# Dealing out the expert work anew in a fused two-layer network: earlier loads, a row of ones on another engine, and a band stage that starts in halves

## The chip, the cores and the metric

The program runs on one core of one Trainium2 chip. The time is device microseconds of one launch. The unchanged kernel took 1212.18 us as the median of three runs (1210.66 to 1214.54). Engines are named as in the profile: PE is the matmul engine, DVE the vector engine, ACT the scalar engine, POOL the GpSimd engine, SP the engine that here only issues DMAs.

## The reference, cut to what matters

Two layers over x of shape (4, 512, 128). Only the first is touched by the change:

```python
# first layer: windowed attention, 16 heads, a window of 64 earlier tokens
strain = disp_win - disp[:, :, :, None, :]
bond_act = gelu(strain @ W_strain + rel_emb @ W_pos)            # exact gelu
damage_act = gelu(strain @ W_dmg + b_dmg)
damage = sigmoid((damage_act @ W_dmg_out)[..., 0] + b_dmg_out[0])
logits = (bond_act @ W_bond)[..., 0] - 10.0 * damage
out = einsum('bntd,bntde->bnte', softmax(masked logits), val_win) @ W_cproj
# first layer: mixture of 16 experts, each token goes to 4 of them
route = softmax over the top 4 of t @ gate_w.T + gate_b
acc += route[e] * (swiglu(t @ mlp1_w[e].T + b1[e]) @ mlp2_w[e].T + b2[e])
# second layer: full attention with 16 heads, and 8 experts with 2 per token
```

## The kernel before, in words

The first layer is six blocks one after the other; at the end of a block all engines meet at a barrier. They are: a setup (0 to 40 us), a loop for heads 0 to 7 (`g` = 0, from 40), a band stage for them (from 331), the same loop for heads 8 to 15 (`g` = 1, from 414), its band stage (from 682), and then, from 776, the second layer.

**The loop.** A loop works through 64 window positions ("items"), 8 to each of its 8 iterations `it`. For one item DVE forms the two strained inputs (`strain`, L757, one of 2.2 us for the bond and one for the damage half), ACT takes the gelu (L895, or L900, L901 and L903), and PE reduces the result to logits (`reduce`, L957) and gives back the ring buffer. In 5 of 8 items PE forms the damage half instead of DVE (`strain` of PE, L981 and L985) from a bf16 copy `DS` of the input in three parts, whose partitions 96 to 98 hold ones for a bias. At the start of each loop DVE and ACT split the input in three parts (L863, L870, L935, L937), SP copies them to `DS` (12 DMAs, L669), and POOL writes the ones (L732). At the end of each half iteration ACT takes a tanh of the logits (`tanh`, L911).

**Experts between the items.** The expert rows of the first layer lie in 20 groups of 512 rows, sorted by expert. POOL scatters the rows of all tokens to them by 64 indirect DMAs (L741) during the first loop. A group then takes these steps: SP loads its rows (`tokens`, L649) and its weights (`weights1`, L656; `weights2`, L663); PE turns the rows (`turn`, L1019); DVE copies them (`move_in`, L813); PE multiplies by the first weights (`hidden`, L1027); DVE adds the bias (`glu_in`, L821), ACT takes a tanh (`sig`, L917), DVE combines (`glu_out`, L828); PE multiplies by the second weights (`expert_out`, L1036); DVE copies the result out (`move_out`, L835); and POOL works out where the rows go (`goals`, L712 to L718) and scatters them by 4 indirect DMAs (`store`, L723). An iteration has room for two groups, A and B_. The table `MOE_ITS` says which iterations have groups: 5, 6 and 7 of the first loop (groups 0 to 5), and 0 to 6 of the second (groups 6 to 19). The `turn` of an iteration's A stands at the end of the iteration before. SP issues all of these DMAs in the order in which they are written, so a wait of one holds back the rest. At the end of the second loop SP waits for all stores and starts to load the results back (`fetch`, L592).

**The band stage.** Four blocks `k` of 128 tokens. PE turns the logits, DVE subtracts the maximum (L1163, L1165), ACT takes the exponential into `zs` (`weigh`, L1212), SP writes `zs` to DRAM (`write`, L1138, 1 MB), and SP and POOL read it back shifted by one token per row (`read`, L1121, SP the first 64 rows of a block, POOL the others). Then PE turns what came back (`turn`, L1298), DVE and ACT copy it (L1174, L1238), and PE gathers the values (L1316, L1324). For block 0 the exponential is taken in two halves of the groups of heads (`parts_of`), but the write and the read are whole. Before block 0's turn PE fills its time with `keep_busy` (L151, 20 matmuls), which works on nothing.

Of the kernel before, what the change touches and what calls it, by code (L numbers as in the profile page):

```python
# [20 lines left out]
P = 128  # L21
# [4 lines left out]
WIN = 64  # L26
# [34 lines left out]
MOE_ITS = ((5, 6, 7), (0, 1, 2, 3, 4, 5, 6))  # L61
# [41 lines left out]
def moe_groups(g, it):  # L103

    if it not in MOE_ITS[g]:
        return None, None
    first = 2 * (len(MOE_ITS[0]) * g + MOE_ITS[g].index(it))
    return first, first + 1
# [79 lines left out]
def first_layer(nc, t_in, l0, sb, psum, sem, ident, ACC, nhalf, stats, mv, rstd, carried):  # L188
# [55 lines left out]
    with ExitStack() as su:  # L244
# [333 lines left out]
        sem(n) for n in ("moe_turned", "moe_moved", "h_ready", "xg_ready", "sig_ready", "s_ready", "y_ready", "y_used"))  # L578
    d_scatter, d_w2, goals_ready = sem("d_scatter0"), sem("d_w2_"), sem("goals_ready")
# [34 lines left out]
    for g in range(G):  # L614
        with ExitStack() as lp:
# [25 lines left out]
            groups = [n for it in MOE_ITS[g] for n in moe_groups(g, it)]  # L641

            @block.sync
            def _(sp):
# [20 lines left out]
                sp.wait_ge(small_pool, 5 + 2 * g)  # L665
# [15 lines left out]
                first, end = groups[0], groups[-1] + 1  # L681
                weights1(first)
# [16 lines left out]
                for n in range(2):  # L699
                    sp.wait_ge(d_ys[n], 64 * (end // 2))  # L700
# [5 lines left out]
            def _(pool):  # L706
# [25 lines left out]
                pool.memset(DS[96:99], 1.0).then_inc(small_pool, 1)  # L732
                pool.wait_ge(small_pool, 6 + 2 * g)
# [17 lines left out]
            def _(v):  # L751
# [85 lines left out]
                def body(it):  # L837
                    A, B_ = moe_groups(g, it)
                    before = moe_groups(g, it - 1)[1]
# [44 lines left out]
            def _(act):  # L884
# [33 lines left out]

                def body(it):
# [1466 lines left out]
```

## Time and profile before

| | |
|---|---|
| median of three runs | 1212.18 us |
| the profiled execution | 1208.67 us, of which its span is 1206.9 us |
| mean granted clock of PE | 0.928 of full speed |
| PE, DVE, ACT, POOL busy | 83%, 75%, 65%, 48% of the span |

The profiled execution is 3.5 us below the median of the runs. Times in the rows further down are microseconds from the start of its span. A row of the timeline reads: start, time, engine, line, operation, what it writes and reads, how often in a row, and in brackets how long its engine had stood idle before it and what ended that.

### The profile page before, as it was taken

To read this page: it belongs to the slowest core of one execution; us is meant where nothing else is said; L and a number is where in the kernel's file an instruction comes from. 1 tells how busy PE (TensorE), PEld (TensorE's weight loads), DVE (VectorE), ACT (ScalarE), POOL (GpSimd) and SP (SyncE) were. 2 spreads that over 40 slices of the span, in tenths; PEclk is the share of its full clock that TensorE was granted. 3 is DMA by queue.
4 is the path that set the end of the run, shared out by engine and by line. 5 is a ranking of instruction groups with operands and counts; after the bars stand their busy time and mean duration, and the time that the engine had idled before them with its cause. 6 is when DMAs were issued, how large, how long until landed. Compare 5 with 4: busy or idle time off the path is not lost. (4 is left out here: it accounts for less than half of the span.)

```text
span 1206.9 us, 24564 instructions
## 1 busy us (share of the span) xinstructions
PE 998.7 (83%) x9762; PEld 543.5 (45%) x9762; DVE 905.2 (75%) x1050; ACT 781.6 (65%) x840; POOL 573.5 (48%) x568
## 2 busy tenths in 40 slices
PE   6677787699569649999998687899999999999898
PEld 3422222233268514433333386753654565646533
DVE  7888788599363579999999674667768577576756
ACT  3589999599453459999999652143156666665464
POOL 5598888258555234888887510232760000000072
PEclk9779999799879869999999978999879999999999
DMA  8470100112157132222221396000132344522121
GB/s 302 122 271 32 36 31 31 45 49 67 38 161 188 24 84 59 72 73 70 70 70 33 100 254 142 24 1 1 36 105 62 105 132 124 155 84 84 47 59 45
DMA packets 117101, 105.14 MB, mean 87 GB/s; under 512 B 11551, under 2 KB 103419, under 8 KB 116347
## 3 DMA queue, kind: packets, MB, share of 16 engines
q1 hardware_dynamic: 106968, 83.24, 24.4%
q0 software_dynamic: 8448, 20.13, 5.9%
q8 instruction: 77, 1.26, 0.5%
q10 hardware_dynamic: 1571, 0.20, 0.1%
q14 instruction: 37, 0.30, 0.1%
HBM read 62.05 MB, written 38.34 MB: 83 GB/s over the span
## 5 line engine op out<-in xcount | busy, mean ns | idle before, releaser
L757 DVE SCALAR_TENSOR_TENSOR ring<-AD,PT 128x1808 f32<-128x1808 f32 (+15 forms) x128 | 282.1, 2221 | 33.2 <-PE LG L957 30.8
L957 PE MATMUL LG<-ring,lred 128*32 128x456 f32 (+15 forms) x2048 | 242.9, 595 | 17.6 <-ACT ring L895 17.6
L723 POOL DMA_INDIRECT ys<-yo,goali x80 | 168.5, 2107 | 77.8 <-DVE yo L835 54.7
L895 ACT ACTIVATE ring<-ring 128x3616 f32<-128x3616 f32 (+15 forms) x52 | 177.3, 3410 | 14.9 <-DVE ring L757 14.8
L2222 DVE TENSOR_REDUCE MX<-SS 128x2 f32<-128x1024 f32 x119 | 144.5, 1218 | 55.8 <-PE SS L1939 55.7
L2152 ACT ACTIVATE EX<-SS 128x1024 f32<-128x1024 f32 x128 | 130.4, 1031 | 78.9 <-PE SS L1939 78.4
L741 POOL DMA_INDIRECT xs<-rows,sloti x64 | 142.5, 2227 | 23.7 <-issue 19.2
L981 PE MATMUL SD<-DS,eyes 99*32 99x456 bf16 (+14 forms) x1216 | 92.0, 379 | 61.4 <-ACT ring L900 61.0
L901 ACT ACTIVATE ring<-ring 128x1824 f32<-128x1824 f32 (+14 forms) x76 | 139.0, 1829 | 0.0
L1856 POOL DMA_INDIRECT XN<-ys,sloti x16 | 16.2, 1015 | 248.0 <-PE SS L1949 243.5
L957 PEld LDWEIGHTS LG<-ring,lred 128*32 128x32 f32 x2048 | 62.0, 113 | 122.5 <-issue 93.3
L757 DVE SCALAR_TENSOR_TENSOR ring<-AD,bdmg 128x1808 f32<-128x1808 f32 (+15 forms) x52 | 114.8, 2207 | 0.0
L900 ACT ACTIVATE ring<-SD 128x912 f32<-128x912 f32 (+14 forms) x76 | 74.7, 983 | 33.6 <-PE SD L985 32.7
L981 PEld LDWEIGHTS SD<-DS,eyes 99*32 99x32 bf16 x1216 | 21.4, 96 | 158.3 <-ACT ring L900 101.2
L985 PE MATMUL SD<-DS,eyes 96*32 96x456 bf16 (+14 forms) x1216 | 90.9, 374 | 0.0
L903 ACT ACTIVATE ring<-SD 128x912 f32<-128x912 f32 (+14 forms) x76 | 74.9, 985 | 10.7 <-PE SD L985 10.6
L1939 PE MATMUL SS<-KS,QS 32*128 32x512 f32 x238 | 62.2, 516 | 14.8 <-DVE MX L2222 12.9
L1959 PE MATMUL PW<-EX,VA 128*32 128x512 f32 x512 | 69.0, 612 | 0.0
L2129 ACT ACTIVATE HB<-PHh,b1c 128x128 f32<-128x128 f32 x156 | 44.8, 371 | 37.0 <-PE PHh L1891 36.8
L1939 PE MATMUL SS<-QS,KS 32*128 32x512 f32 x256 | 65.4, 511 | 3.4 <-ACT EX L2152 2.1
L2274 DVE RECIPROCAL attT<-attT 128x128 f32<-128x128 f32 (+1 forms) x58 | 54.4, 959 | 0.2
L1212 ACT ACTIVATE zs<-wtT 128x2048 f32<-128x2048 f32 (+1 forms) x10 | 31.9, 3192 | 24.1 <-DVE wtT L1165 14.9
(407 smaller groups left out, 1739.8 us busy)
## 6 DMA issues: line engine op xcount, KB each, us to landing
w1s<-in_L_ffn_W SPq DMA_DIRECT2D x39, 256.0 KB, 3.0
w2s<-in_L_ffn_W SPq DMA_DIRECT2D x39, 256.0 KB, 2.9
band<-zs SPq DMA_DIRECT2D x8, 1024.0 KB, 10.8
wide<-band POOLq DMA_DIRECT2D x16, 380.0 KB, 8.3
wide<-band SPq DMA_DIRECT2D x16, 380.0 KB, 11.2
xl<-xs SPq DMA_DIRECT2D x20, 272.0 KB, 3.0
xs<-Z SPq DMA_DIRECT2D x5, 1024.0 KB, 8.8
w1s<-w1d SPq DMA_DIRECT2D x80, 64.0 KB, 1.8
```

The lines of the kernel that those rows point to most:

```text
L723: pool.indirect_dma_start(ys0[:, :], bass.IndirectOffsetOnAxis(ap=goali[:, 4 * n + a:4 * n + a + 1], axis=0), yo[:, n % 2, a, :], None, bo ...
L741: pool.indirect_dma_start(xs0[:, :], bass.IndirectOffsetOnAxis(ap=sloti[:, t, k:k + 1], axis=0), rows[:, t, :], None, bounds_check=ROWS0 - ...
L757: return v.scalar_tensor_tensor(out=ring[:, slot, s, :, t0:T], in0=AD[:, s, :, j + t0:j + T], scalar=extra, in1=AD[:, s, :, PAD + t0:PAD + T],
L895: act.activation(tiles, tiles, ACT.Gelu).then_inc(gelu_done, 1)
L901: act.activation(tiles, tiles, ACT.Gelu)
L903: act.activation(ring[:, slot, 1, 2:4, t0:T], SD[:, :, t0:T], ACT.Gelu).then_inc(gelu_done, 1)
L957: mm = pe.matmul(LG[32 * b:32 * b + 32, par, s, t0:T], lred[:, s, n % 4, :], ring[:, slot, s, b, t0:T], start=(n % 4 == 0), stop=(n % 4 == 3))
L981: pe.matmul(SD[32 * q:32 * q + 32, i, t0:T], eyes[0:99, q, :], DS[0:99, q, 2 * half + i, j + t0:j + T], start=True, stop=False)
L985: mm = pe.matmul(SD[32 * q:32 * q + 32, i, t0:T], eyes[0:96, 4, :], DS[0:96, q, 2 * half + i, PAD + t0:PAD + T], start=False, stop=True)
L1939: mm = pe.matmul(bank[:, n, :], rows[r:r + 32, b % 2, q, P * t:P * t + P], cols[r:r + 32, b % 2, q, :], start=True, stop=True)
L2152: act.activation(EX[:, Q % 2, hh:hh + 2, t, :], SS[:, slot, :, :], ACT.Exp, scale=SCALE1).then_inc(freed[slot], 1)
L2222: v.tensor_reduce(MX[:, t, p // 2, hh:hh + 2], pairs_of(b, name), AX.X, ALU.max).then_inc(freed[slot], 1)
```

## The change

There are four edits.

1. The groups are dealt anew by a table `MOE`. The first loop has group 0 as B_ of iteration 5, groups 1 and 2 in iteration 6 and group 3 as A of iteration 7. The second loop has group 4 ahead of its first iteration (`ahead`), groups 5 to 18 in iterations 0 to 6, and group 19 as A of iteration 7. ACT gets a `move_in` and a `move_out` for the group ahead.
2. In the second loop SP loads the rows of groups 4 and 5 and the first weights of group 4 before it copies the parts to `DS`. After that it goes through the groups one by one.
3. The ones in `DS` are written by ACT in four copies (`ones_row`), not by POOL in one.
4. In the band stage block 0 is written to DRAM and read back in two halves by groups of heads. SP reads back the first half ahead of the write of block 1. PE waits for the halves one by one.

```diff
-MOE_ITS = ((5, 6, 7), (0, 1, 2, 3, 4, 5, 6))
+MOE = ({5: (None, 0), 6: (1, 2), 7: (3, None)},
+       {-1: (None, 4), **{it: (5 + 2 * it, 6 + 2 * it) for it in range(7)}, 7: (19, None)})
...
 # SP, the loop
+                first, end = groups[0], groups[-1] + 1
+                if g:
+                    tokens(first)
+                    tokens(first + 1)
+                    weights1(first)
-                sp.wait_ge(small_pool, 5 + 2 * g)
+                sp.wait_ge(small_pool, 5 + g)
                 for n, ready, count in ((0, parts_act, 1), (1, parts_act, 2), (2, parts_dve, 2)):
...
-                weights1(first)
+                if g == 0:
+                    weights1(first)
                 weights1(first + 1)
                 weights2(first)
                 if g == 0:
                     sp.wait_ge(d_scatter, 16 * TT * K0)
-                tokens(first)
-                tokens(first + 1)
-                for n in range(first, end, 2):
-                    if n > first:
-                        weights2(n)
+                    tokens(first)
+                    tokens(first + 1)
+                for n in groups:
                     if n + 2 < end:
                         weights1(n + 2)
                         tokens(n + 2)
-                        weights1(n + 3)
-                    weights2(n + 1)
-                    if n + 2 < end:
-                        tokens(n + 3)
+                    if n + 1 < end:
+                        weights2(n + 1)
...
 # POOL
-                pool.memset(DS[96:99], 1.0).then_inc(small_pool, 1)
 # DVE, ahead of the first iteration
+                glu_in(ahead)
                 item(1, 0)
                 if g == 0:
                     tile_tables()
+                glu_out(ahead)
                 item(2, 0)
 # ACT
+                def ones_row(q):
+                    act.copy(DS[96:99, q].rearrange("p b t -> p (b t)"), lones[96:99, 0, 0:1].to_broadcast([3, B * TP])).then_inc(ones_ready, 1)
...
                 act.copy(parts[0], AD[:, 1, :, PAD:PAD + T]).then_inc(parts_act, 1)
+                move_in(ahead)
                 act.wait_ge(parts_dve, 2 * g + 1)
                 act.copy(parts[1], rest).then_inc(parts_act, 1)
+                ones_row(0)
                 gelu(0, 0)
+                sig(ahead)
+                ones_row(1)
+                ones_row(2)
                 gelu(1, 0)
+                ones_row(3)
+                move_out(ahead)
 # PE
+                turn(ahead)
+                hidden(ahead)
                 reduce(0, 0)
+                expert_out(ahead)
                 turn(moe_groups(g, 0)[0])
...
 # the band stage: SP
                 write(0)
-                for k in range(1, NT):
+                read(sp, 0, 0, 0)
+                write(1)
+                read(sp, 0, 0, 1)
+                for k in range(2, NT):
                     write(k)
                     read(sp, k - 1, 0)
 # write(k) and read(k) go over the parts of a block
+                    for part, (f, l) in enumerate(parts_of(k)):
+                        sp.wait_ge(ex_ready, 5 * g + (k + 2 if k else part + 1))
+                        sp.dma_start(band[k].rearrange("p (g r) -> p g r", g=NG)[:, f:l, 0:4 * WIN],
+                                     zs[:, k % 2, f:l].rearrange("p g s n -> p g (s n)")).then_inc(written(k, part)[0], 16)
```

What stands in a row on PE in the first loop, around the end of iteration 4 (`L1019` is the turn of group 0, `L957` a reduction, `L981` and `L985` the strained inputs that PE forms). Before:

```order
L957 MATMUL LG0<-ring0,lred 32x488 [waits gelu_done]
L957 MATMUL LG0<-ring0,lred 32x488 x7
L1019 MATMUL PH0<-ident,xl0 128x128 [waits xg_ready,d_xl_0_]
L1019 MATMUL PH0<-ident,xl0 128x128 x3
L981 MATMUL SD0<-DS0,eyes 32x492 [waits sd_taken]
L981 MATMUL SD0<-DS0,eyes 32x492 x7
```

And in the changed kernel, in iteration 5 (its turn is `L1044`, the strained inputs are `L1006` and `L1010`, and `L981` is its reduction):

```order
L981 MATMUL LG0<-ring0,lred 32x492 [waits gelu_done]
L981 MATMUL LG0<-ring0,lred 32x492 x7
L1006 MATMUL SD0<-DS0,eyes 32x496 [waits gelu_done]
L1006 MATMUL SD0<-DS0,eyes 32x496 x7
L1010 MATMUL SD0<-DS0,eyes 32x496 x8
L1044 MATMUL PH0<-ident,xl0 128x128 [waits xg_ready,d_xl_0_]
L1044 MATMUL PH0<-ident,xl0 128x128 x3
L1006 MATMUL SD0<-DS0,eyes 32x496 [waits sd_taken]
L1006 MATMUL SD0<-DS0,eyes 32x496 x7
```

The turn of group 0 has moved back by three reductions and what stands between them.

The start of the second loop on ACT. Before:

```order
L935 CAST ring1<-AD 128x4x512
L937 CAST ring1<-ring1 128x4x512 [waits parts_dve]
L895 ACT_TABLE_LOAD
L895 ACTIVATE ring1<-ring1 128x8x452 [waits strain_ready] x4
L900 ACTIVATE ring1<-SD1 128x2x456 [waits sd_ready,strain_ready]
```

And now (`L924` is the `move_in`, `L934` the ones, `L919` the `sig` and `L931` the `move_out` of the group ahead, `L897` the gelu):

```order
L952 CAST ring1<-AD 128x4x512
L924 COPY attT<-PH1 128x512 [waits moe_turned]
L955 CAST ring1<-ring1 128x4x512 [waits parts_dve]
L934 CAST DS1<-lones 3x2304
L897 ACT_TABLE_LOAD
L897 ACTIVATE ring1<-ring1 128x8x452 [waits strain_ready]
L919 ACTIVATE attT<-xg1 128x512 [waits xg_ready]
L934 CAST DS1<-lones 3x2304 x2
L897 ACTIVATE ring1<-ring1 128x8x452 [waits strain_ready]
L934 CAST DS1<-lones 3x2304
L931 COPY yo1<-PY1 128x512 [waits d_ys_0_,y_ready]
L897 ACTIVATE ring1<-ring1 128x8x452 [waits strain_ready] x2
```

Seven instructions have come in ahead of the third gelu, two of which wait for PE.

The start of the second loop on PE, now (`L1052` is `hidden`, `L1061` is `expert_out`); before, only `L957`, the wait at `L1019` and the reduction of item 1 stood here:

```order
L1044 MATMUL PH1<-ident,xl1 128x128 [waits xg_ready,d_xl_0_]
L1044 MATMUL PH1<-ident,xl1 128x128 x3
L1052 MATMUL PH1<-attT,w1s1 128x128 [waits d_w1_0_,moe_moved]
L1052 MATMUL PH1<-attT,w1s1 128x128 x3
L981 MATMUL LG1<-ring1,lred 32x452 [waits gelu_done,banks_free]
L981 MATMUL LG1<-ring1,lred 32x452 x7
L1061 MATMUL PY1<-w2s1,xg1 128x128 [waits y_used,d_w2_,s_ready]
L1061 MATMUL PY1<-w2s1,xg1 128x128 x3
L1044 MATMUL PH1<-ident,xl1 128x128 [waits xg_ready,d_xl_1_]
L1044 MATMUL PH1<-ident,xl1 128x128 x3
L981 MATMUL LG1<-ring1,lred 32x452 [waits gelu_done]
```

The whole of group 4's work on PE now lies around the first reduction.

## Rows read from the trace of the kernel before

**Rows 1.** Busy time by stage: us, then each engine, clock, DMA share.

```profile
40.00:331.10 291.10, 217.67 (x2432) 82.15 (x2432) 233.06 (x179) 235.72 (x165) 213.74 (x145) 0.90 0.23 71
414.00:681.70 267.70, 217.97 (x2520) 90.31 (x2520) 246.44 (x206) 240.12 (x173) 191.77 (x172) 0.95 0.26 71
```

**Rows 2.** Timeline of ACT: the tanh that ends a half iteration.

```profile
169.09 0.66 ACT L911 ACTIVATE Z<-LG,bdo 128x476 f32<-128x476 f32 x1
199.37 0.67 ACT L911 ACTIVATE Z<-LG,bdo 128x484 f32<-128x484 f32 x1
242.84 0.68 ACT L911 ACTIVATE Z<-LG,bdo 128x492 f32<-128x492 f32 x1
306.40 0.69 ACT L911 ACTIVATE Z<-LG,bdo 128x508 f32<-128x508 f32 x1
...
545.12 0.66 ACT L911 ACTIVATE Z<-LG,bdo 128x476 f32<-128x476 f32 x1
575.82 0.67 ACT L911 ACTIVATE Z<-LG,bdo 128x484 f32<-128x484 f32 x1
670.16 0.69 ACT L911 ACTIVATE Z<-LG,bdo 128x508 f32<-128x508 f32 x1
```

**Rows 3.** The scatter's end, PE's turn of group 0, scatter durations (minimum, median, maximum).

```profile
215.24 0.97 POOL L741 DMA_INDIRECT xs<-rows,sloti  x1 [0.30 <-issue]
220.54 1.12 PE L1019 MATMUL PH<-ident,xl 128*128 128x128 f32 x4 [10.98 <-DMA xl<-xs]
...
L741 POOL DMA_INDIRECT xs<-rows,sloti x64: 967/1840/15899, 54.5 to 215.2; - x64
```

**Rows 4.** Timeline of all engines at the end of both loops.

```profile
307.55 1.16 PE L1027 MATMUL PH<-attT,w1s 128*128 128x128 f32 x8
310.75 0.68 DVE L835 COPY yo<-PY 128x512 f32<-128x512 f32 x1
312.28 1.10 POOL L723 DMA_INDIRECT ys<-yo,goali  x1 [1.69 <-DVE yo L835]
316.61 0.97 POOL L723 DMA_INDIRECT ys<-yo,goali  x1 [0.31 <-issue]
331.14 10.41 POOL L1127 MEMSET wide<- 128x4096 f32 x3 [7.50 <-POOLq L615]
...
671.46 0.80 SPq L592 DMA_DIRECT2D rows<-ys  x1
681.71 10.44 POOL L1127 MEMSET wide<- 128x4096 f32 x3 [11.68 <-POOLq L615]
```

**Rows 5.** Timeline of POOL, DVE and ACT at the start of the first loop.

```profile
41.24 7.77 POOL L732 MEMSET DS<- 3x9216 bf16 x1
44.36 1.90 ACT L937 CAST ring<-ring 128x2048 bf16<-128x2048 f32 x1 [2.46 <-DVE ring L863]
44.63 4.46 DVE L785 TENSOR_SCALAR attT<-attT 16x128 f32<-16x128 f32 x1
64.56 3.22 ACT L895 ACTIVATE ring<-ring 128x3616 f32<-128x3616 f32 x1 [1.10 <-DVE ring L757]
```

**Rows 6.** Timeline of SP, PE and ACT at the start of the second loop.

```profile
416.04 9.42 SPq L669 DMA_DIRECT2D DS<-ring  x12
438.95 0.94 SPq L649 DMA_DIRECT2D xl<-xs  x2
441.99 1.12 PE L1019 MATMUL PH<-ident,xl 128*128 128x128 f32 x4 [13.86 <-DMA xl<-xs]
447.78 0.93 ACT L900 ACTIVATE ring<-SD 128x912 f32<-128x912 f32 x1 [9.80 <-PE SD L985]
```

**Rows 7.** Timeline of PE in the two band stages.

```profile
360.70 1.23 PE L1298 MATMUL WB<-ident,wide 128*128 128x128 f32 x8 [1.26 <-DMA wide<-band]
709.47 1.24 PE L1298 MATMUL WB<-ident,wide 128*128 128x128 f32 x8
741.50 0.42 PE L1324 MATMUL ZT<-wtT,vp 128*32 128x64 f32 x3 [6.57 <-issue]
```

More of the change, by code:

```diff
@@ L103, in moe_groups @@
 def moe_groups(g, it):
[L105 to L108, printed above, removed]
+    return MOE[g].get(it, (None, None))
 def dram_rows(tensor, offset, dims):
@@ L640, in first_layer @@
             PYf = PY[:].rearrange("p n c -> p (n c)")
-            groups = [n for it in MOE_ITS[g] for n in moe_groups(g, it)]
+            groups = [n for it in sorted(MOE[g]) for n in MOE[g][it] if n is not None]
+            ahead = moe_groups(g, -1)[1]
             @block.sync
@@ L838, in body @@
                     A, B_ = moe_groups(g, it)
-                    before = moe_groups(g, it - 1)[1]
+                    before = moe_groups(g, it - 1)[1] if it else None
                     move_in(A)
@@ L1110, in summed, with written, landed, read @@
                 return ZT[:, 8:12, :] if k % 2 else WB[:, 3]
-            def read(engine, k, half):
+            def written(k, part):
+                if k == 0 and part == 0 or 0 < k < NT - 1:
+                    return d_out[k], 16 * (g + 1)
+                return d_out[NT - 1], 32 * g + (32 if k else 16)
+            def landed(k, part, half):
+                each = 16 * (64 // BLK)
+                if k == 0 and part == 0 or 0 < k < NT - 1:
+                    return d_in[k][half], each * (g + 1)
+                return d_in[NT - 1][half], 2 * each * g + (2 * each if k else each)
+            def read(engine, k, half, only=None):
                 engine.wait_ge(wide_zero, (WIDE + 1) * g + min(k, WIDE - 1) + 1)
-                engine.wait_ge(d_out[k], 16 * (g + 1))
                 if k >= WIDE:
                     engine.wait_ge(band_pe, 8 * (M0 + k - WIDE + 1))
-                for s0 in range(0, 64, BLK):
-                    r0 = 64 * half + s0
-                    rows = dram_rows(band, (k * P + r0) * 32 * P, [[32 * P - 4, BLK], [4 * P, NG], [1, 4 * SPAN]])
-                    engine.dma_start(wide[r0:r0 + BLK, k % WIDE, :, s0:s0 + SPAN, :].rearrange("r g s n -> r g (s n)"), rows
-                                     ).then_inc(d_in[k][half], 16)
+                for part, (f, l) in enumerate(parts_of(k)):
+                    if only not in (None, part):
+                        continue
+                    engine.wait_ge(*written(k, part))
+                    for s0 in range(0, 64, BLK):
+                        r0 = 64 * half + s0
+                        rows = dram_rows(band, (k * P + r0) * 32 * P + 4 * P * f, [[32 * P - 4, BLK], [4 * P, l - f], [1, 4 * SPAN]])
+                        engine.dma_start(wide[r0:r0 + BLK, k % WIDE, f:l, s0:s0 + SPAN, :].rearrange("r g s n -> r g (s n)"), rows
+                                         ).then_inc(landed(k, part, half)[0], 16)
             @block.gpsimd
@@ L1208, in weigh @@
                     if k >= 2:
-                        act.wait_ge(d_out[k - 2], 16 * (g + 1))
+                        for part in range(len(parts_of(k - 2))):
+                            act.wait_ge(*written(k - 2, part))
                     for f, l in parts_of(k):
```

31 lines of the change are left out of this document (21 added, 10 removed).

## The prediction

> **What bounds the kernel now.** I read the busy time by stage first, then the timeline of each engine where two stages meet, and last the waits inside the loops. In both loops ACT is the busiest of the engines that every item passes (235.72 of 291.10 us and 240.12 of 267.70 us, [rows 1]), but the first loop is 23 us longer than the second with fewer experts in it: it has holes. The tanh rows date them [rows 2]. A full iteration takes 199.37 - 169.09 = 30.28 us without experts, and at the same place of the second loop, with two groups, 575.82 - 545.12 = 30.70 us. So a group costs 0.21 us there: it lies under the items. The iteration after 199.37 takes 43.47 us. There PE stands 10.98 us at the turn of group 0, until its rows have landed [rows 3]; they can't be loaded before POOL has ended its 64 scatters (the last starts at 215.2). At the end of the first loop the last group's stores hold the barrier: the next stage starts at 331.14, 7.50 us after POOL's last store, and 331.14 - 306.40 = 24.74 us after the last tanh but one [rows 2, 4]. The second loop has no such tail: POOL had been idle for 11.68 us, and the next stage starts 681.71 - 670.16 = 11.55 us after that tanh. So much the items need by themselves. At its start, though, PE waits 13.86 us for rows which SP issues at 438.95, behind 12 copies to the parts and 12 weights [rows 6].
>
> **The change part by part.** The sum is made against the profiled execution, 1208.67 us, 3.5 us below the median.
>
> *Turn of group 0, first loop.* It moves from the end of iteration 4 to the middle of iteration 5, and iteration 5 keeps one group of two. Without the hole the iteration is 30.28 us times 492/484 (the columns of its tanh rows), 30.8, and 0.2 for a group: 31.0 against 43.47. That is **-12.5 us**. The cover: the turn would be reached some 24 us after 199.37 less what the start gains, about 222 to 224; the rows land at 220.5 or a little earlier. The scatter decides this. Its median duration is 1840 ns; the last one, in the hole where PE and the engines behind it stand still, takes 0.97 us, near the shortest [rows 3]. In the changed kernel the hole isn't there, so the last four or five may take 0.9 us more each; that is 4 us at most, against about 3 of room. Cost taken: 0, bound +3.
>
> The Trainium skill (SBUF — State Buffer, section "Who interferes with whom") says that a DVE instruction with two SBUF inputs gets in the way only of GpSimd work that reads SBUF, and not, by inference, of its writing of descriptors. By that rule the scatters wouldn't care whether DVE works, and the room of 3 us would be whole. The trace, with a median of 1840 ns beside a DVE full of exactly such instructions, rather speaks against it, and the trace decides; the sum is the same by both.
>
> *Tail of the first loop.* The last group is now the A of iteration 7. Without B_ its second matmul starts where `hidden` of B_ stood, 307.55, and ends near 308.7; the copy (0.68) ends at 309.4; POOL starts 0.85 us later, as it did (310.75 + 0.68 to 312.28), needs 5.30 us for four stores (312.28 to 316.61 + 0.97) and then the 7.50: 323.0 against 331.14 [rows 4]. **-8.1 us**. This takes the 7.50 as something that follows POOL's last indirect DMA whatever else is done.
>
> *Tail of the second loop.* Group 19 is the A of iteration 7 here too. The same path gives a next stage at 323.0 - 306.40 = 16.6 us after the tanh, where it was 11.55: **+5.1 us**. This is the part of the change that loses. SP's loads of the results, which followed the stores at 671.46 [rows 4], move behind as well, to about 681, still ahead of the stage that uses them; I take nothing for them. Bounds: 0 (if the end is set by the items) to +8.
>
> *Start of the first loop.* POOL's write of the ones lasts 7.77 us, and DVE's small TENSOR_SCALAR which starts under it takes 4.46 us and ends with it, at 49.09 [rows 5]. Without it DVE has some 4 us more, but then waits for PE's counting matmuls, and ACT gets four copies. Each has 2304 elements in a row; at the pace of the cast of 2048 (1.90 us) that is 2.14 us, 8.6 us in all. The first starts at 44.36 + 1.90 = 46.26, ahead of the first gelu; two lie between the first and the second gelu and one behind that, where ACT waited for DVE, and by this chain the last ends near 62.6 to 63.4, where the third gelu, now at 64.56, can follow. Behind that everything is 1 to 2 us earlier. I take **-2.0 us**; the ends are -4.5 (DVE's whole stall) and +4.1 (8.6 less 4.46).
>
> *Start of the second loop.* SP now issues the rows (0.94) and four weights first. The 12 weights took 438.95 - 425.46 = 13.5 us, 4.5 for four [rows 6]. Then come 12 copies (9.42 us with their waits for the parts, some 7 without) and 8 weights: the second weights of group 4 are issued by about 436 and land at 437 to 438, since rows issued by 439.89 had landed at 441.99. `expert_out` of group 4 waits for them in PE's order, and the turn of group 5 follows at about 439.5, 2.5 us before the turn it replaces (441.99). ACT meanwhile has the 8.6 us of ones and three operations for group 4, 2.0 us at the 0.67 of the tanh rows, and waits for `expert_out` before the third gelu. By that it reaches the first gelu from PE at 446.5, where it was 447.78: **-1.3 us**. Behind the wait of ACT's `move_out` stand the gelus of items 2 and 3, and PE's reductions wait for those. The ends: -9.8 us (ACT's whole wait before that gelu goes) and +3 us (the weights land that much later).
>
> *Band stage in halves.* In the first stage PE's turn of block 0 waits 1.26 us for the read-back, 29.56 us after the stage's start; in the second it doesn't wait at all and stands at 27.76 us [rows 7]. `keep_busy` fills the rest, so no more than the 1.26 us can go: **-1.3 us** in the first, 0 in the second. The two extra writes and eight extra read DMAs are small and on queues that wait anyway. The second stage now starts after an idle tail, as the first always did, so I give it the first stage's 29.56 - 1.26 = 28.3 against 27.76: **+0.5 us**.
>
> Sum: -12.5 - 8.1 + 5.1 - 2.0 - 1.3 - 1.3 + 0.5 = **-19.6 us**. From the profiled execution that is 1189.1 us, from the median 1192.6 us. Medians being what is compared, I say **1191 us**.
>
> **The rivals.**
>
> *The tail isn't POOL's.* The 7.50 us stand in one place only. After the second loop's stores (POOL idle from 681.71 - 11.68 = 670.03) SP went on at 671.46, 1.4 us later, when they had landed. If the rest was an accident of the first barrier, the stages end with the items or with SP: the first loop near 318, 5 us earlier than I say, and the second near 684, 3 us earlier, without the +0.5. Against it: the page names no other releaser for that barrier. Time: 1191 - 8.5 = 1182.5 us.
>
> *The copies of ones aren't hidden.* ACT is the engine that every item waits for. If the starts of the loops come out at their upper ends, +4.1 and +3, where I have -3.3, the time is 1191 + 10.4 = 1201 us. For it: ACT waits in its order for PE twice in the second. Against it: ACT stood idle for 9.80 us there [rows 6].
>
> *The stall comes back.* If the scatter's end slides, turn of group 0 waits again, 3 to 5 us: 1195 us.
>
> *Slower: PE starved of its instructions in the band stages.* At 741.50 PE had waited 6.57 us for nothing that the profile shows, in the middle of 128 equal matmuls, while SP's queue was full of reads [rows 7]. The change puts more DMAs and an earlier read in this stage, and the loads of results later. Each such stall more costs 6.57 us; from four on (26.3 us against 19.6) the kernel is slower: 1217 us. Against it: the bytes are the same, and the eight blocks had one stall of this length.
>
> **How the numbers follow.** My forecast 0.62, its own range 1186 to 1196; tail not POOL's 0.13, 1182.5; ones not hidden 0.14, 1201; stall back 0.07, 1195; starved 0.03, 1217; the last 0.01 is for several gains failing together, near no change. What this measurement can tell from no change is 0.3%, 3.6 us, so faster means below 1208.5. All cases but the last two are: faster 0.95, same 0.02 (one stall or two more on top of the ones), slower 0.03. The range has to take in the tail case and most of the ones case: 1181 to 1202.
>
> **What the changed profile would show.** Right: no wait of PE for `xl` in the first loop; the tanh at 492 columns 31 us after the one at 484; POOL idle about 7.5 us before the first memset of both band stages, and the second one's start some 16.6 us after the tanh at 508 columns; DVE's small TENSOR_SCALAR well under 1 us; ACT's four casts of 3x2304 at 2.1 us each. Wrong: a new wait of PE at `expert_out` of group 4 much beyond 439, a second loop whose full iterations with experts take longer than 30.7 us at 484 columns, or stalls of PE without a releaser of over 5 us in more than one block of a band stage.

## The result: 1190.14 us, and where the time went

The changed kernel took **1190.14 us** (median of 4 runs, 1185.18 to 1192.71), the kernel before 1213.36 us beside it. The ratio is **0.9835** (95% interval 0.9803 to 0.9867), 1.65% faster. The forecast was 1191 us. Its profiled execution took 1192.71 us, with a span of 1191.0; before they were 1208.67 and 1206.9. The kernel before took 1208 and 1213 us in two series of runs and 1260 to 1264 us in three others, so each time below stands with its ratio to the kernel before in its own series.

The tanh rows of ACT again date the loops; they answer to [rows 2].

```profile
76.54 0.64 ACT L913 ACTIVATE Z<-LG,bdo 128x452 f32<-128x452 f32 x1
194.88 0.67 ACT L913 ACTIVATE Z<-LG,bdo 128x484 f32<-128x484 f32 x1
225.62 0.68 ACT L913 ACTIVATE Z<-LG,bdo 128x492 f32<-128x492 f32 x1
289.17 0.69 ACT L913 ACTIVATE Z<-LG,bdo 128x508 f32<-128x508 f32 x1
428.42 0.64 ACT L913 ACTIVATE Z<-LG,bdo 128x452 f32<-128x452 f32 x1
643.26 0.69 ACT L913 ACTIVATE Z<-LG,bdo 128x508 f32<-128x508 f32 x1
```

The interval in which the hole was, from 484 to 492 columns, is 225.62 - 194.88 = 30.74 us, where it was 43.47. Term by term, in the two profiled executions:

| term | forecast | measured | how |
|---|---|---|---|
| turn of group 0 | -12.5 | **-12.7** | 30.74 for 43.47 |
| tail, first loop | -8.1 | **-9.2** | 304.69 - 289.17 = 15.52 for 24.74 |
| tail, second loop | +5.1 | **+2.6** | 657.45 - 643.26 = 14.19 for 11.55 |
| start, first loop | -2.0 | **-3.1** | 76.54 - 38.79 = 37.75 for 40.84, from POOL's first memset on |
| start, second loop | -1.3 | **-0.6** | 428.42 - 387.46 = 40.96 for 41.58 |
| first band stage | -1.3 | **-0.1** | 82.8 for 82.9 |
| second band stage | +0.5 | **+1.6** | 96.0 for 94.4 |
| sum | -19.6 | **-21.5** | |

The setup took 1.35 us less (38.79 for 40.14). The spans differ by less than all this, 15.9 us, because the second layer, in which nothing was changed, took 437.6 us in this execution and 430.8 in the one before. The same kernel, profiled once more (a_again below), took 430.7 there, and its span is 19.7 us below the one before. So these 7 us belong to the execution and not to the change. Windows of the second layer of the changed kernel, first in this execution, then in the repeated one (PE busy, clock, DMA share, GB/s):

```profile
753.45:1191.00 437.55, 403.21 (x2434) 0.94 0.25 73
```

```profile
756.58:1187.27 430.69, 396.77 (x2434) 0.95 0.26 74
```

The three smallest terms rest on a single profile of the kernel before, while the same work varies between executions. The start of the second loop took 40.8 to 41.7 us in eight that have it unchanged. The first band stage took 78.5 to 82.8 us in seven with halves and 20 idle matmuls, the second 95.6 to 100.3 us in the same seven. So the -0.6 and the -0.1 can't be told from zero, and of the second band stage it can be said only that it was longer than 94.4 in all of them.

**Group 0.** POOL's last scatter, the first instruction of POOL that needs them, and PE's turn, with the durations of all scatters; they answer to [rows 3].

```profile
205.97 2.30 POOL L741 DMA_INDIRECT xs<-rows,sloti  x1 [0.31 <-issue]
213.39 0.21 POOL L713 TENSOR_TENSOR match<-xl,place 128x16 f32<-128x16 f32 x1 [5.12 <-DMA xl<-xs]
221.92 0.66 PE L1044 MATMUL PH<-ident,xl 128*128 128x128 f32 x4
...
L741 POOL DMA_INDIRECT xs<-rows,sloti x64: 968/1822/17927, 50.0 to 206.0; - x64
```

PE turns group 0 at 221.92 without a wait. The rows had landed at 213.39, so the room is 8.5 us here and not the 3 that I counted. The last scatter starts 9.3 us earlier than before: 1.35 of it is the setup, 3.1 come because DVE isn't held up by POOL's write of the ones and gives the scatters their indices sooner (the first starts 11.25 us after POOL's first memset, for 14.33), and 4.9 because the scatters themselves took less, 155.9 us from the first start to the last for 160.8.

**The tails.** The last group's copy, its stores, and the first instruction of the next stage, at the end of both loops; they answer to [rows 4]. The last row, of a view of windows, is the stretch between the last traffic and the barrier (busy time of PE, PEld, DVE, ACT and POOL, clock, DMA share, GB/s).

```profile
291.52 0.69 DVE L835 COPY yo<-PY 128x512 f32<-128x512 f32 x1 [1.62 <-PE PY L1061]
293.05 0.97 POOL L724 DMA_INDIRECT ys<-yo,goali  x1 [2.31 <-DVE yo L835]
296.88 0.97 POOL L724 DMA_INDIRECT ys<-yo,goali  x1 [0.30 <-issue]
304.69 3.51 POOL L1171 MEMSET wide<- 128x4096 f32 x1 [6.84 <-POOLq L614]
...
650.96 0.97 POOL L724 DMA_INDIRECT ys<-yo,goali  x1 [0.30 <-issue]
653.34 0.80 SPq L591 DMA_DIRECT2D rows<-ys  x1
657.45 3.51 POOL L1171 MEMSET wide<- 128x4096 f32 x1 [5.52 <-POOLq L614]
...
299.70:304.60 4.90, 0.00 (x0) 0.00 (x0) 0.69 (x1) 0.02 (x1) 0.00 (x0) 0.74 0.00 0
```

The step that I took as 7.50 us is 6.84 at the first barrier and 5.52 at the second. For the last 4.9 us before the first one no engine but DVE (0.69 us) does anything and no byte moves.

**The starts.** In the first loop DVE's small operation takes 0.27 us instead of 4.46, and ACT's copies of the ones take 2.11 us each, as estimated; they answer to [rows 5]. In the second ACT waits 2.44 us for `expert_out` of group 4, which waits for its weights; this answers to [rows 6].

```profile
43.27 0.27 DVE L785 TENSOR_SCALAR attT<-attT 16x128 f32<-16x128 f32 x1
44.93 2.11 ACT L934 CAST DS<-lones 3x2304 bf16<-3x2304 f32 x1
...
411.75 2.05 PE L1061 MATMUL PY<-w2s,xg 128*128 128x128 f32 x8 [7.11 <-issue]
413.84 0.58 ACT L931 COPY yo<-PY 128x512 f32<-128x512 f32 x1 [2.44 <-PE PY L1061]
```

**The band stage.** PE no longer waits for the read-back, but block 0's turn stands at 334.24, 29.55 us after the stage's start, as before (29.56, [rows 7]). The idle matmuls ahead of it last until then. The read-back itself has moved up. Its last two reads, SP's for the second half, are in the first row (duration in ns, then the starts).

```profile
L1165 SPq DMA_DIRECT2D wide<-band x2: 606/838/1070, 322.5 to 323.1; - x2
DMA to landing us min/median/max: 6.0/6.1/6.2
...
326.90 7.50 PE L149 MATMUL ZT<-ident 128*128 128x128 f32 x40 [0.85 <-DVE wtT L1213]
334.24 1.13 PE L1349 MATMUL WB<-ident,wide 128*128 128x128 f32 x8
```

The second half had landed by 329.3, that is 24.6 us after the stage's start and 4.9 before the turn.

### The profile page after: what moved, and what is told of

Same layout as the page of the kernel before. It is cut to its first block and busy times, and to the rows that moved or that the text cites. A ratio compares the mean times of both kernels' runs of the same rounds, so it can differ in the third digit from the quotient of the medians.

```text
span 1191.0 us, 24584 instructions
## 1 busy us (share of the span) xinstructions
PE 1000.1 (84%) x9762; PEld 547.7 (46%) x9762; DVE 900.3 (76%) x1048; ACT 798.6 (67%) x850; POOL 568.4 (48%) x570
## 3 DMA queue, kind: packets, MB, share of 16 engines
q8 instruction: 77, 1.26, 0.5%
## 5 line engine op out<-in xcount | busy, mean ns | idle before, releaser
L981 PE MATMUL LG<-ring,lred 128*32 128x456 f32 (+15 forms) x2048 | 237.0, 583 | 11.0 <-ACT ring L897 11.0
L724 POOL DMA_INDIRECT ys<-yo,goali x80 | 164.9, 2061 | 80.3 <-DVE yo L835 46.7
L897 ACT ACTIVATE ring<-ring 128x3616 f32<-128x3616 f32 (+15 forms) x52 | 177.1, 3410 | 0.2
L741 POOL DMA_INDIRECT xs<-rows,sloti x64 | 139.0, 2172 | 28.5 <-issue 19.2
L1006 PE MATMUL SD<-DS,eyes 99*32 99x456 bf16 (+14 forms) x1216 | 91.2, 376 | 69.0 <-ACT ring L902 68.8
L981 PEld LDWEIGHTS LG<-ring,lred 128*32 128x32 f32 x2048 | 60.9, 111 | 111.1 <-issue 81.5
L1006 PEld LDWEIGHTS SD<-DS,eyes 99*32 99x32 bf16 x1216 | 21.0, 95 | 165.5 <-ACT ring L902 109.6
L1010 PE MATMUL SD<-DS,eyes 96*32 96x456 bf16 (+14 forms) x1216 | 89.7, 370 | 0.0
L1926 PEld LDWEIGHTS PW<-w2s,HB 128*128 128x128 f32 x312 | 39.0, 195 | 19.5 <-issue 11.1
```

The lines of the kernel that those rows point to most:

```text
L724: pool.indirect_dma_start(ys0[:, :], bass.IndirectOffsetOnAxis(ap=goali[:, 4 * n + a:4 * n + a + 1], axis=0), yo[:, n % 2, a, :], None, bo ...
L741: pool.indirect_dma_start(xs0[:, :], bass.IndirectOffsetOnAxis(ap=sloti[:, t, k:k + 1], axis=0), rows[:, t, :], None, bounds_check=ROWS0 - ...
L897: act.activation(tiles, tiles, ACT.Gelu).then_inc(gelu_done, 1)
L981: mm = pe.matmul(LG[32 * b:32 * b + 32, par, s, t0:T], lred[:, s, n % 4, :], ring[:, slot, s, b, t0:T], start=(n % 4 == 0), stop=(n % 4 == 3))
L1006: pe.matmul(SD[32 * q:32 * q + 32, i, t0:T], eyes[0:99, q, :], DS[0:99, q, 2 * half + i, j + t0:j + T], start=True, stop=False)
L1010: mm = pe.matmul(SD[32 * q:32 * q + 32, i, t0:T], eyes[0:96, 4, :], DS[0:96, q, 2 * half + i, PAD + t0:PAD + T], start=False, stop=True)
```

## The experiments

All edits are to the changed kernel. The series are e1 to e4; a_again and e5 to e7; e9, c1 and c2; and c1 again. Only the second of them holds the changed kernel itself. Kernels are compared within a series, and stages by the profile. In the first, third and fourth the kernel before took 1260 to 1264 us.

### e1: the turn of group 0 back

```diff
-MOE = ({5: (None, 0), 6: (1, 2), 7: (3, None)},
+MOE = ({5: (0, None), 6: (1, 2), 7: (3, None)},
```

> The changed kernel with one entry dealt back: group 0 of the first loop is the first group of iteration 5 again ({5: (0, None), ...}), so its turn stands at the end of iteration 4. Theory: its rows cannot land before the 64 scatters have ended (about 219 to 221 us), and PE has to stand there; the tanh at 492 columns comes 43 us after the one at 484 instead of 30.7, +12 to +12.5 us for the kernel. Rival (the gain came from dealing three groups over other iterations, not from the wait): the interval stays near 31 us and the time within 2 us of the changed kernel.

Measured: 1254.29 us, ratio 0.996 (0.9915 to 1.0004), against 1244.07 and 1248.99 for e3 and e2 of the same series. PE's turn and the tanh rows in this kernel:

```profile
197.20 0.67 ACT L913 ACTIVATE Z<-LG,bdo 128x484 f32<-128x484 f32 x1
217.20 1.11 PE L1044 MATMUL PH<-ident,xl 128*128 128x128 f32 x4 [9.81 <-DMA xl<-xs]
238.72 0.68 ACT L913 ACTIVATE Z<-LG,bdo 128x492 f32<-128x492 f32 x1
```

PE waits 9.81 us again, and the interval is 41.52 us, 10.8 more than 30.74. From the first tanh to the first band stage it takes 240.8 us, and 229.9 in e3. So the mechanism is shown; it is worth 11 us once the rows land earlier, and was worth 12.7 with the old landing.

### e2: POOL writes the ones again

```diff
+                pool.memset(DS[96:99], 1.0).then_inc(small_pool, 1)
-                ones_row(0)   # and the three others on ACT
```

> The changed kernel with the three rows of ones written by POOL's memset again and ACT's four copies gone, in both loops. Theory: DVE's small TENSOR_SCALAR on attT takes 4.4 us again under the memset of the first loop and its first tanh comes 2 to 3 us later; at the second loop's start ACT has 8.6 us less to do, but waits for PE's output of group 4, so it gives nothing there: +2 to +3 us in all. Rival (ACT is what every item waits for, so the copies cost in the second loop): its first tanh comes 2 to 6 us earlier, and the kernel is not slower than the changed one.

Measured: 1248.99 us, ratio 0.9923 (0.9888 to 0.9957). DVE's stall under POOL's write is back, and so is the late scatter:

```profile
43.47 4.47 DVE L786 TENSOR_SCALAR attT<-attT 16x128 f32<-16x128 f32 x1
...
216.08 0.97 POOL L742 DMA_INDIRECT xs<-rows,sloti  x1 [0.30 <-issue]
221.27 2.11 POOL L713 TENSOR_TENSOR match<-xl,place 128x16 f32<-128x16 f32 x1 [4.22 <-DMA xl<-xs]
223.77 0.66 PE L1040 MATMUL PH<-ident,xl 128*128 128x128 f32 x4
```

The first loop's first tanh comes 78.29 - 38.98 = 39.31 us after POOL's first memset; in the three other kernels of this series it is 37.8. So the ones are worth **1.5 us** there. At the start of the second loop they are worth nothing: 41.05 us with POOL's ones, 41.05 in e3 with ACT's. The medians, 4.9 us apart, have overlapping intervals and can't weigh so small a term. The other 1.5 us of the 3.1 between the two kernels are PE's clock in the execution of before, at the same place of the work (PE busy, clock, DMA share, GB/s; first before, then e2):

```profile
74.00:78.00 4.00, 3.62 (x36) 0.71 1.01 410
```

```profile
73.00:77.00 4.00, 2.90 (x48) 1.00 1.02 411
```

The edit has a second effect that I had not put into the sum. With POOL's ones the first scatter starts 14.34 us after POOL's first memset, with ACT's 10.8 to 12.5 us after it. The rows of group 0 land at 221.27 here and the turn comes at 223.77: 2.5 us of room, about the 3 that I had counted. But not all of the difference to 8.5 is the edit. In eleven profiled executions with ACT's ones and group 0 in the middle of iteration 5 the last scatter started between 205.1 and 213.5 us, the room was 3.4 to 12.3 us (3.4 in e5, 5.0 in e4 and e7), and PE never waited, nor did it in e2. The edit starts the scatters some 3 us sooner, and the turn comes 1.5 us sooner by it too, so it adds about 1.6 us of room. The rest is how long the scatters take: 153 to 162 us with ACT's ones, 162.8 in e2.

What makes them differ can be read from the trace. Rows of POOL and DVE in the changed kernel:

```profile
194.12 0.97 POOL L741 DMA_INDIRECT xs<-rows,sloti  x1 [0.30 <-issue]
197.37 2.26 DVE L757 SCALAR_TENSOR_TENSOR ring<-AD,bdmg 128x1968 f32<-128x1968 f32 x1
198.60 1.88 POOL L741 DMA_INDIRECT xs<-rows,sloti  x1 [0.30 <-issue]
```

The first scatter runs while DVE is idle, and takes 0.97 us. The second ends at 200.48, 0.85 us after DVE's strain has ended at 199.63. That is so for all of them: of the 896 scatters in the fourteen profiled executions 165 took 0.97 to 0.98 us, and each of the other 731, which took 1.68 us or more, ended 0.83 to 0.87 us after the end of a DVE instruction. At the start of 717 of these a strain had been running for over 0.1 us, at the start of the short ones never. So DVE's strains hold the scatters up, as the prediction suspected. How many are caught differs: 15 were short in e6 (153.1 us in all) and 10 in e4 and e7 (161.3 us). The Trainium skill (SBUF — State Buffer, "Who interferes with whom") says by inference that a DVE instruction with two SBUF inputs doesn't hold up the writing of descriptors; for these indirect DMAs, which take their indices from SBUF, the measurement says otherwise, and it decides. No run took DVE's work away to try it by itself.

### e3, e7 and e9: the halves and the idle matmuls

e3 writes and reads block 0 whole, and SP reads it back behind the write of block 1 again; e7 keeps the halves and has fewer idle matmuls; e9 has both edits. The first is shown in short.

```diff
-                for part, (f, l) in enumerate(parts_of(k)):
+                for part, (f, l) in enumerate(((0, NG),)):
-                keep_busy(pe, ZT[:, 0, :], ident, 20)
+                keep_busy(pe, ZT[:, 0, :], ident, 9)
```

> The changed kernel with block 0 of both band stages written and read back whole again. Theory (from the changed kernel's trace): PE's fixed number of idle matmuls ahead of block 0 hides the read-back almost entirely, so block 0's turn stays within 0.1 to 1.3 us of 29.5 us after the stage's start, in both stages: 0 to +1.3 us. Rival (the halves cost, by ten more DMAs on SP and POOL): the second stage, which is 1.6 us longer in the changed kernel, goes back to 94.4 us.

> The changed kernel with 9 instead of 20 of the idle matmuls that PE does ahead of block 0 in both band stages. Theory (they hide what the halves gain): block 0's turn moves from 29.5 and 28.8 us after the stage's start to 26 to 28 us, when the first half has landed and ACT's last Exp ends, -1.5 to -3 us a stage, -3 to -6 in all. Rival (the idle matmuls hold the clock up): PE waits instead, its granted clock in the 30 us behind falls, and the stages get no shorter or even longer.

> Block 0 written and read back whole, as in e3, with 9 instead of 20 idle matmuls ahead of it, as in e7. Theory (the idle matmuls covered most of what the halves give): PE now waits for the read-back of the whole block, which lands some 28.6 to 29.4 us after the stage's start, so block 0's turn stands there instead of at 26.0 and 25.1 us, and both stages together are 5 to 7 us longer than in e7: the halves are worth 2.5 to 3.5 us a stage, once the cover is gone. Rival (the halves give nothing, the idle matmuls alone were the cost): the turn comes at 25 to 26 us here too, and the time is that of e7.

Measured: e3 1244.07 us (0.9886, 0.9823 to 0.9949); e7 1182.61 us (0.9775, 0.9721 to 0.9828), beside 1190.39 for the changed kernel; e9 1247.75 us (0.9911, 0.9877 to 0.9945). PE's turn of block 0, or the matmuls ahead of it, in e3 (both stages), e7 (first) and e9 (both):

```profile
337.97 1.23 PE L1347 MATMUL WB<-ident,wide 128*128 128x128 f32 x8 [0.76 <-DMA wide<-band]
696.14 1.10 PE L1347 MATMUL WB<-ident,wide 128*128 128x128 f32 x7 [0.65 <-DMA wide<-band]
```

```profile
327.36 4.21 PE L149 MATMUL ZT<-ident 128*128 128x128 f32 x18 [2.52 <-DVE wtT L1213]
331.36 1.54 PE L1349 MATMUL WB<-ident,wide 128*128 128x128 f32 x8
```

```profile
335.64 1.13 PE L1347 MATMUL WB<-ident,wide 128*128 128x128 f32 x4 [3.06 <-DMA wide<-band]
694.32 0.91 PE L1347 MATMUL WB<-ident,wide 128*128 128x128 f32 x3 [3.26 <-DMA wide<-band]
```

After the stage's start this is:

| | 20 idle | 9 idle |
|---|---|---|
| whole | 29.35 and 29.37, waits 0.76 and 0.65 | 29.31 and 29.43, waits 3.06 and 3.26 |
| halves | 29.00 and 28.71 (a_again) | 25.98 and 25.13 |

With the block whole the read-back sets the turn, and taking idle matmuls away only lengthens the wait. With halves and 20 idle matmuls these set it; in the seven profiled executions of that kind it stood at 27.8 to 29.7 us in the first stage and 26.9 to 28.8 in the second. With 9 idle matmuls the halves move it by 3.3 and 4.3 us. Even there PE doesn't wait for the read-back, so this is the least that the halves are worth; the landing itself moved from about 29.5 us in the kernel before to 24.6.

The rival of e7, a lower clock behind, did not show: over the 30 us behind the turn the granted clock was 0.98 and 0.94 in e7, and 0.94 in both stages of a_again. The whole first stage lasted 76.3 us in e7 (75.8 and 76.4 in the two runs of c1, 81.0 in e9). In seven profiled executions with halves and 20 idle matmuls it lasted 78.5 to 82.8 us, mostly by PE's clock and its short stops without a releaser. So the -0.1 us in my table means little, and the turn's place is the better measure. In the second stage e7's gain at the turn is largely given back later: PE's last long wait for DVE ends 85.4 us after the start there and 85.8 in a_again, and the stages last 96.6 and 97.2 us. Both stages together took 172.9 us in e7 and 179.5 in e9, 6.5 apart, as expected, though single stages differ by up to 5 us between executions.

### e4 and e5: what holds the barrier at a loop's end

e4 leaves out the last group's stores and SP's waits for them. e5 moves PE's second matmul of this group ahead of one reduction.

```diff
# e4
-                    store(n)
+                    if n < groups[-1]:
+                        store(n)
# e5, and none behind hidden(B_) in iteration 7
+                    if it == 7:
+                        expert_out(A)
                     reduce(4, it)
```

> The changed kernel without the four indirect stores of the last group of each loop (groups 3 and 19), and with SP's four loads of results reading the same number of bytes from another tensor; so the sum over the experts is left out of the output. The matmuls and copies of these groups stay. Theory (the last stores hold the barrier): both band stages start about 0.3 us after DVE's last instruction of the loop, that is 11.5 us after the tanh at 508 columns, where they start 15.5 and 14.2 us after it: -4.0 and -2.7 us, -6.7 us in all. Rival (the barrier is held by something else, such as the sequencers' next instructions): 15.5 and 14.2 us stay, no change.

> The changed kernel with PE's second matmul of the last group (in iteration 7 of both loops) ahead of reduce(4), as soon as DVE has its input ready, instead of behind it. Theory (the last stores hold the barrier, a fixed time behind them): the copy moves up from behind PE to behind DVE's last item, 1.6 us, and both band stages start 1.6 us earlier after the tanh at 508 columns (13.9 and 12.6 us instead of 15.5 and 14.2), -3.2 us in all, with POOL's idle time before them again 6.84 and 5.52 us. Rival (what ends POOL's idle time is not counted from its last store): these idle times grow by what the stores gain, and the stages start as before.

Measured: e4 1234.93 us (0.9824, 0.9764 to 0.9883), e5 1181.16 us (0.9763, 0.972 to 0.9805) beside 1190.39 for the changed kernel. The first instructions of the stages, in e4 and then in e5:

```profile
302.36 6.97 POOL L1174 MEMSET wide<- 128x4096 f32 x2 [10.65 <-POOLq L614]
302.39 1.94 PE L1314 MATMUL ZT<-ident,Z 128*128 128x128 f32 x16 [1.80 <-PEq L614]
...
655.84 6.97 POOL L1174 MEMSET wide<- 128x4096 f32 x2 [10.64 <-POOLq L614]
```

```profile
303.52 3.51 POOL L1174 MEMSET wide<- 128x4096 f32 x1 [6.84 <-POOLq L614]
...
650.88 6.97 POOL L1174 MEMSET wide<- 128x4096 f32 x2 [5.52 <-POOLq L614]
650.92 1.94 PE L1314 MATMUL ZT<-ident,Z 128*128 128x128 f32 x16 [2.74 <-PEq L614]
650.88:655.88 5.00, 3.69 (x32) 1.00 0.89 296
```

Without the stores the stages start 11.56 and 11.55 us after the tanh at 508 columns, against 15.52 and 14.19. That is the 11.55 which the second loop had before, where the items end it. So the stores hold both barriers, for 4.0 and 2.6 us. With the stores earlier the tails are 13.81 and 12.50 us, 1.7 shorter each, and POOL's idle time stays at 6.84 and 5.52. It has these two values, to 0.01 us, in all eight profiled executions with the changed kernel's last stores and in e5 (c1 and c2 have 6.84 and 5.9); what makes one longer than the other stays open. e5's median lies 9.2 us below the changed kernel's, and the tails are 3.4 of it; another 3.2 are in its first band stage, where other executions differ as much without the edit.

The same rows show what a late start costs the second band stage at first. PE's 16 transposes at the stage's start take 1.94 us where PE had been idle for 1.80 or 2.74 us. In the changed kernel PE had been idle for 4.44 us before its second stage, and the clock over the first 5 us is 0.70 (the window above is e5's, at 1.00, with the same DMA share):

```profile
657.45:662.45 5.00, 4.96 (x32) 0.70 0.89 296
```

ACT's first exponential comes 5.95 us after the start there, 4.53 in e4, e5 and in the kernel before (686.24 - 681.71). Of these 1.4 us 1.0 is still there at block 0's turn, at 28.83 us after the start, 27.81 in e5 and 27.76 before. The results' loads, which now run into this stage, are not the cause of that: they do so in e5 too. At the stage's end nothing of it can be seen: it lasted 96.0 us in the changed kernel, 97.0 in e5 and 98.3 in e4, which both started at the full clock. So the clock at the start doesn't explain the 1.6 us of my table, and their cause stays open.

### e6: the second weights of group 4 first

```diff
+                if g:
+                    weights2(first)
                 weights1(first + 1)
-                weights2(first)
                 if g == 0:
+                    weights2(first)
```

> The changed kernel with SP's four second weights of group 4 issued ahead of the four first weights of group 5 in the second loop. Theory (PE's 7.1 us wait at expert_out of group 4 is for these weights, and ACT's copy behind it comes 2.4 us late): the wait falls to about 3 us, ACT's wait of 2.44 us goes, and the tanh at 452 columns of the second loop comes 2.0 to 2.4 us earlier (38.6 to 39.0 us after the loop's start instead of 41.0). Rival (ACT's third gelu waits for the parts or for DVE anyway): the tanh stays within 0.5 us.

Measured: 1188.49 us (0.9836, 0.9793 to 0.9879).

```profile
404.63 2.04 PE L1063 MATMUL PY<-w2s,xg 128*128 128x128 f32 x8 [2.90 <-issue]
417.32 3.06 PE L983 MATMUL LG<-ring,lred 128*32 128x452 f32 x16
421.27 0.93 ACT L904 ACTIVATE ring<-SD 128x912 f32<-128x912 f32 x1 [2.16 <-PE SD L1012]
417.30:420.30 3.00, 3.00 (x24) 0.54 0.29 87
```

ACT's wait at the copy is gone, and its first gelu from PE comes 30.62 us after the loop's start (384.63), 2.9 earlier than in a_again (33.54). But 6 us later ACT waits 2.16 us for PE. There PE had run the reduction ahead of it in 3.06 us, at a granted clock of 0.54. c1 has the same edit, and there the clock was 1.00 at this place:

```profile
413.24 1.69 PE L983 MATMUL LG<-ring,lred 128*32 128x452 f32 x16
415.96 0.93 ACT L904 ACTIVATE ring<-SD 128x912 f32<-128x912 f32 x1 [0.61 <-PE SD L1012]
```

The tanh comes after 39.90 us in e6 and after 40.10 in the second run of c1, where the wait is 2.15 us; with the wait at 0.61 it comes after 38.20 us in c1 and 38.49 in c2. Where the weights come in the old order it took 40.8 to 41.7 us. So the edit gives some 2.3 to 3.5 us where the clock is full, more than the 2 to 2.4 expected, and PE's clock took some 1.6 back in two of the four executions. The rival (the tanh stays within 0.5 us) was wrong.

### a_again, c1 and c2: the changed kernel once more, and better ones

c1 joins the edits of e5, e6 and e7; c2 has 4 instead of 12 idle matmuls ahead of block 1 as well.

> The changed kernel itself, as the measure for the others of this call, which run on the same chip. On the chip of the first four experiments every kernel took some 4% longer, and the second loop's iterations with two groups took about 0.8 us more each than on the first chip. Theory (the chip's clock, not the change): ratio to the kernel before 0.980 to 0.987 here as well, with the first loop's tail at 15.5 us and the turn's interval at 30.7 us. Rival (the second loop suffers from the change on such a chip, as it has one group more): the second loop is over 2 us longer than before, and the ratio over 0.987.

> The changed kernel with the edits of e5 (second matmul of the last group earlier), e6 (second weights of group 4 ahead) and e7 (9 idle matmuls) together. Each by its stages: -3.4, -1.3 and -5 to -6 us. If they add up, 10 us less than the changed kernel: a ratio near 0.976 to the kernel before. Rival (they share a cover): only the largest is left, near 0.980.

> The kernel of c1 with 4 instead of 12 idle matmuls ahead of block 1 too. PE has an idle time of 2.8 us without a releaser in the middle of these 12, and two runs of matmuls of some 3.2 us in all beside it. Theory (block 1 has landed by then, the idle matmuls are a plain cost): -2 to -4 us a stage against c1. Rival (block 1's read-back or the clock ends the wait): the stages stay within 1 us.

> The kernel of c1 once more, with more rounds, since its first run fell on a chip on which the kernels with two groups an iteration lose 0.8 us in each iteration. Theory (the three edits add up, by stages -3.4, -1.3 and -5 to -6 us against the changed kernel): 1180 us where the changed kernel takes 1190, a ratio near 0.976, or near 0.978 on a chip like that of its first run. Rival (only e7's part counts): 0.980 or more.

Measured: a_again 1190.39 us, ratio 0.9848 (0.98 to 0.9897), with a first tail of 15.52 us and the turn's interval as before; so the change gives the same again. Its second loop is 2.6 us longer than before, which is the tail's +2.6. c1 1233.64 us, 0.9779 (0.9701 to 0.9856), and with more runs 1232.11 us, **0.974 (0.971 to 0.977)**. That is clearly faster than the kernel before. It lies below the changed kernel's intervals (0.9803 to 0.9867, and 0.98 to 0.9897) too, but the two were never timed in one series, so that c1 beats the changed kernel is likely and not shown; and as e5 alone has 0.972 to 0.9805, it isn't shown either that the three gains add up. c2 1234.9 us, 0.9787 (0.9715 to 0.986): no gain over c1, where 2 to 4 us a stage were expected. Block 0's turn of the first stage stands at 25.1 us in both; c2's two stages are 4.0 and 2.0 us longer, the first with a stop of 4.56 us of PE, without a releaser, in the middle of its matmuls.

## Why the prediction was right, and which terms were off

*The number.* 1191 us was forecast and 1190.14 measured. That it came within 1 us is partly luck. The terms are off by up to 2.5 us each and by 1.9 together, the setup took 1.35 us less, and 1191 lies between the 1189.1 from the profiled execution and the 1192.6 from the median. Both large terms came out by their mechanism: the turn's stall (-12.7 for -12.5), shown by e1, and the first tail (-9.2 for -8.1), shown by e4 and e5.

*Turn of group 0.* The cost of 0 was right, and so was the suspicion that a scatter takes longer beside DVE's work. But the room was taken too small: I let the rows land "at 220.5 or a little earlier", and missed that POOL's write of the ones stood in front of the scatters' indices. Without this edit the room was 2.5 us in e2, with it 3.4 to 12.3 us. The edit accounts for some 1.6 us of that, and no run shows PE waiting without it.

*The tails.* The step "7.50 us after POOL's last store, whatever else is done" was the right mechanism with a wrong size: 6.84 and 5.52 us. Stores of 4.80 us instead of 5.30 make the rest of the difference. The rival that the tail isn't POOL's fell with e4.

*Start of the first loop.* The term was -2.0; the edit gives -1.5, and another 1.5 us were the clock in the one execution from which I read the time before.

*Start of the second loop.* The order of events was right (`expert_out` of group 4 waits for its weights, ACT behind it). The size was not: SP issued these weights at 406.6 to 410.2, and PE went on at 411.75, 24.3 us after the loop's start, where my estimate was 437 to 438 less 414.0, some 23.5. ACT's first gelu from PE came 33.2 us after it, for 32.5 by the forecast, and so -1.3 came out as -0.6. Other executions of the same start give +0.1 to -0.8 against the one of before, so even the sign is hardly shown.

*Band stage in halves.* The step "no more than the 1.26 us can go" held, but nearly nothing went. I had named `keep_busy` as what fills the time and did not ask what it would do when the wait behind it is gone. e3, e7 and e9 show it: the halves are worth at least 3.3 and 4.3 us of the turn's place with 9 idle matmuls, and with 20 they remove the 0.76 us that PE waits in e3 (1.26 in the kernel before); the rest of the turn's place is then set by the idle matmuls and the clock.

*Second stage's start.* I gave it +0.5 us at block 0's turn for starting after an idle tail. There it was 1.1 (28.83 for 27.76), through PE's clock at the stage's start. The +1.6 of the whole stage is not explained by it; its cause stays open.

*The slower rival* (PE starved of its instructions) did not show: the stops without a releaser in the band stages are 2.90 and 0.97 us in the first and 3.98 us as the longest in the second, where 6.57 was the longest before.

*Range.* Both ends held, and the rivals at 1182.5 and 1201 us fell for the reasons above.

## What to carry to other kernels

Filler work with a fixed length hides an improvement of the transfer that it was put in front of: when that transfer is made earlier, shorten the filler in the same edit, and judge the two together. An indirect store near a barrier cost its own time and 5.5 to 7.5 us behind it here, so the last one belongs as far ahead of the last item as its input allows. When a wait is removed by a new order, ask of every edit in the same change what it does to the thing waited for; here moving the ones started the scatters 3 us sooner. Before a wait is put down to a queue, read PE's granted clock in the same stretch: in e6 it was the clock.

## What the runs showed of the hardware

- From the end of POOL's last indirect DMA to the first instruction behind the barrier it took 6.84 us at one barrier and 5.52 us at the other (7.50 at the first in the kernel before, 5.9 at the second in c1 and c2), and where it was looked at, 4.9 us of it were without traffic.
- A scatter of POOL took 0.97 us at the least. Where it took longer, it ended 0.83 to 0.87 us after the end of a DVE instruction, in 731 of 731 cases. The 64 scatters of one program took between 153 and 163 us from the first start to the last, with the same data.
- PE's clock after an idle time: after 1.80 and 2.74 us the first 16 transposes took 1.94 us (granted clock 1.00, the 2.4 GHz level); after 2.80 us (c1's first stage, second run) 3.54 us, after 4.44 us 3.35 us, after 5.77 us 3.65 us (0.67, 0.70 and 0.59 over the stage's first 5 us, so partly at the 1.2 GHz level). In the other executions they took 2.94 to 3.65 us, after 2.79 to 13.90 us of idle. That delays ACT's first exponential by 1.0 to 1.7 us in a stage that starts behind a late store.
- The unchanged second layer took 431 us at a mean granted clock of 0.95 in a_again and 483 us at 0.89 in e9.
